# Two-layer graph attention on one core: the constant offset of layer 0's scores, written by ScalarE instead of by a product of ones

## What is computed

```
h = max(layernorm(x), 0)
x = x + L0(h, adj);  h = max(layernorm(x), 0);  x = x + L1(h, adj)

L0: e = (h Ws) (h Wt)^T ; z = where(adj > 0, e, -9e15) ; h' = softmax(z) (h Wc)
L1: Wh = h W ; e = leaky_relu(s1[:, None] + s2[None, :]) ; masked softmax ; elu(softmax @ Wh)
```

## Time and profile before

| | |
|---|---|
| median of 3 runs | 1403.41 us (1398.08 to 1406.76) |
| span of the profiled execution | 1402.6 us |
| busy: TensorE matmul, VectorE, ScalarE | 1276.6, 1250.6, 1024.8 us (91%, 89%, 73%) |
| DMA engines | 363.10 MB moved |

### The profile page before, as it was taken

How to read it: one execution, slowest core, us unless ns; L and a number is a source line. 1 busy time by engine, 2 the same in 40 slices (tenths; PEclk the granted TensorE clock), 3 DMA queues, 4 the chain that set the end, 5 groups by cost and what they waited for, 6 DMA issues and landing times.

```text
span 1402.6 us, 76097 instructions
## 1 busy us (share of the span) xinstructions
PE 1276.6 (91%) x31819; PEld 1131.9 (81%) x31947; DVE 1250.6 (89%) x2323; ACT 1024.8 (73%) x2036; POOL 32.3 (2%) x75
## 2 busy tenths in 40 slices
PE   5867899999999999999999999989899999999996
PEld 3656788888888888878878888877799999999995
DVE  8877799999999999989999999847899999999996
ACT  5755576767667677667676666748789999999994
POOL 2200000000000000000000000013000000000000
PEclk9979899999999999999999999999899999999998
DMA  6678899999999999999999999531134244334322
GB/s 249 248 266 287 280 345 369 370 381 368 368 391 357 377 378 366 383 380 341 382 378 361 376 374 374 223 114 55 56 108 121 81 124 123 108 94 123 117 85 72
DMA packets 104081, 363.10 MB, mean 259 GB/s; under 512 B 11520, under 2 KB 36352, under 8 KB 70144
## 3 DMA queue, kind: packets, MB, share of 16 engines
q1 hardware_dynamic: 103936, 361.02, 71.2%
HBM read 319.03 MB, written 41.94 MB: 257 GB/s over the span
## 4 chain that ended last, share of the span: by engine, by line
PE 46%; DMA 18%; DVE 16%; issue 12%; ACT 5%; SPq 1%; DVEq 1%; ACTq 0%; POOL 0%; POOLq 0%
DMA arena<-in_adjB 18%; PE ps L883 16%; PE ps L857 9%; DVE arena L1490 5%; PE ps L769 4%; DVE arena L1465 4%; PE ps L764 3%; PE ps L737 3%; DVE mx L1499 2%; ACT arena L1132 2%; PE ps L790 2%; PE ps L725 2%; PE ps L763 1%; PE ps L664 1%; SPq L434 1%
## 5 line engine op out<-in xcount | busy, mean ns | idle before, releaser
L790 PE MATMUL ps<-arena 128*128 128x129 f32 x2048 | 249.0, 280 | 0.4 <-issue 0.4
L1118 ACT ACTIVATE arena<-ps 128x512 f32<-128x512 f32 x256 | 153.2, 598 | 129.8 <-PE ps L737 129.8
L883 PE MATMUL ps<-arena 128*128 128x129 f32 x2048 | 245.1, 278 | 0.4 <-issue 0.4
L790 PEld LDWEIGHTS ps<-arena 128*128 128x128 f32 x2048 | 240.6, 196 | 0.6 <-issue 0.6
L1465 DVE TENSOR_SCALAR arena<-arena 128x2048 fp8e4<-128x2048 int32 x192 | 234.9, 1224 | 3.5 <-PE ps L752 1.5
L883 PEld LDWEIGHTS ps<-arena 128*128 128x128 f32 x2048 | 236.8, 194 | 0.5 <-issue 0.5
L1708 DVE TENSOR_SCALAR arena<-arena 128x128 f32<-128x128 f32 x768 | 202.4, 339 | 19.5 <-issue 14.3
L1112 ACT ACTIVATE arena<-ps 128x512 f16<-128x512 f32 x256 | 153.9, 601 | 52.5 <-PE ps L725 52.3
L769 PEld LDWEIGHTS ps<-arena 128*128 128x128 f16 x2048 | 137.5, 99 | 62.0 <-issue 2.2
L1499 DVE TENSOR_REDUCE mx<-ps 128x1 f32<-128x1024 f32 x128 | 155.7, 1216 | 29.9 <-PE ps L769 29.3
L737 PE MATMUL ps<-arena 128*32 128x128 f16 x8192 | 165.3, 223 | 16.5 <-issue 10.7
(11 more groups left out here) (165 smaller groups left out, 1400.4 us busy)
## 6 DMA issues: line engine op xcount, KB each, us to landing
arena<-in_adjB SPq DMA_DIRECT2D x256, 1024.0 KB, 7.3
sel_pick<-arena SPq DMA_DIRECT2D x64, 256.0 KB, 9.6
sel<-arena SPq DMA_DIRECT2D x64, 256.0 KB, 9.5
arena<-sel_pick SPq DMA_DIRECT2D x64, 256.0 KB, 3.8
arena<-sel SPq DMA_DIRECT2D x64, 256.0 KB, 2.8
arena<-in_xB SPq DMA_DIRECT2D x4, 1024.0 KB, 6.1
x_t<-in_x SPq DMA_DIRECT2D x64, 64.0 KB, 8.0
x_mid<-y_t SPq DMA_DIRECT2D x64, 64.0 KB, 8.3
```

Of the source, the lines that this page charges most:

```text
L790: last = nc.tensor.matmul(pv_ps, p_T[:, s * P:(s + 1) * P], v_sel[:, b, s, :], start=False, stop=(s == SB - 1), skip_group_check=True)
L883: last = nc.tensor.matmul(xv_ps[b], w_msk[:, b, s, :], x1_sel[:, b, s, 0:VW], start=False, stop=(s == SB - 1), skip_group_check=True)
```

## The change

From the second tile on, the product of ones is gone. ScalarE writes -2 OFF over the two banks it has just read, with a Copy of scale 0 and a constant bias, in place (`seed`), straight after each `exps`. TensorE's scores wait for `seeded` where they waited for `p_done`, and the mask product adds to what ScalarE wrote (`start=False`). The first tile keeps the product of ones. A semaphore `seeded` is added.

```diff
-                wait(pe, p_done, t * 2 + (q // 2 - 1))
                 dst = s_ps[q]
-                nc.tensor.matmul(dst, ones_b[:, :], negc, start=True, stop=False, skip_group_check=True)
+                if isinstance(t, int) and t == 0:
+                    nc.tensor.matmul(dst, ones_b[:, :], negc, start=True, stop=False, skip_group_check=True)
+                else:
+                    pe.wait_ge(seeded, t * 2 + (q // 2 - 1))
+                    settle()
                 nc.tensor.matmul(dst, off_i[q // 3], m_sel8[:, b, 4 * q:4 * q + 4, :].rearrange("p s n -> p (s n)"),
                                  start=False, stop=False, skip_group_check=True)
...
+            def seed(t, h):
+
+                act.wait_ge(p_done, t * 2 + (h + 1))
+                dst = ps[:, 2 * h:2 * h + 2, :].rearrange("p b n -> p (b n)")
+                nc.scalar.activation(dst, dst, ACT.Copy, bias=-2.0 * OFF, scale=0.0).then_inc(seeded, 1)
...
                 if there(i, 3):
                     exps(c, 0)
+                    seed(c, 0)
                 if there(i, 2):
                     take_values(a, b, 0)
                     take_keys(a, 3)
                 if there(i, 3):
                     exps(c, 1)
+                    seed(c, 1)
```

More of the change, by code:

```diff
@@ L283, in gnn_kernel @@
         p_done = sem("p_done")
+        seeded = sem("seeded")
         pv_done = sem("pv_done")
```

## The result

The changed kernel takes 1440.3 us (median of 4, 1439.2 to 1442.7) against 1404.0 us (median of 4): a ratio of 1.025, 95% interval 1.022 to 1.029. It is slower by 36 us; 1405 was forecast.

What follows compares the result with a forecast made beforehand. The prediction took memory traffic at 372 GB/s to fill the 13.01 us tile. Its sum was 1402.6 + 0 + 1 + 1 = 1404.6 us on the profiled span, 1405 on the median, own range 1400 to 1411, chance 0.60.

Steps and rivals of the forecast that it cites:

- What bounds the kernel: Steady tile of layer 0: memory traffic alone, 4.85 MB at 372 GB/s, was said to fill the 13.01 us.
- The second cover: Queue of DMA transfers: 4.1 us queued at the next tile's first issue, 3.3 after the change, so the tile stays 13.01.
- The first cover: ScalarE's wait for chunk 3's landing, 1.38 us a tile, was to absorb the 0.87 us longer lap, leaving 0.51.
- The walk of the path: One tile followed through ScalarE, TensorE and VectorE: two seeds of 1.03 us make the lap 0.87 us longer.
- the signs: What the new profile would show, such as seeds of 1.03 us, tiles of 13.0 us and DMA share 0.99.
- Removal of the product of ones: On TensorE: 252 products gone, 55 us of work or 0.88 us a tile, worth nothing by itself.
- The small terms: Steady tiles with short landing waits +1 us, laps behind the last landing +1, early tiles 0.
- Rival 1: Lap of ScalarE and TensorE: seed of 1.29 us or more outlasts the landing wait; nearly all near 1431 us; chance 0.10.
- Rival 2: Irregular landings and a thin DMA queue cost 0.1 to 0.3 us a tile, 1410 to 1422 us; chance 0.19.
- Rival 3: Less TensorE work shortens VectorE's wait for scores: faster, 1385 to 1399 us; chance 0.08.
- Rival 4: Mask product overwrites ScalarE's constant in PSUM: wrong rows at 1405 us, or many times longer in dense form; chance 0.03.

Runs made afterwards that it cites:

- dbl_b: The kernel before the change, with a second buffer for chunk 3 and its transfer issued right behind chunk 0: 1379.3 us, ratio 0.982.
- dbl_mid: The changed kernel with two buffers for chunk 3, which is issued behind chunk 1 and ahead of chunk 2: 1380.9 us, ratio 0.987.
- h1: The changed kernel with seeds for banks 2 and 3 only; banks 0 and 1 keep the product of ones: 1403.0 us, ratio 0.999.
- work2: The kernel before the change, plus two seed-sized copies a tile on ScalarE into SBUF that no other engine waits for: 1427.1 us, ratio 1.020.
- h0: The changed kernel with seeds for banks 0 and 1 only; banks 2 and 3 keep the product of ones: 1445.0 us, ratio 1.027.

## Why the prediction was wrong

**What bounds the kernel** was the step that failed first: "the memory traffic alone fills the tile". The prediction multiplied the tile by 372 GB/s and found the bytes that a tile moves. But 372 was measured in this tile: bytes over a rate taken from the same stretch give the stretch back, whatever binds. dbl_b moves the same bytes at 383 GB/s and dbl_mid at 386. The loop of 25.9 us in two tiles had been read off the chain and was the answer: 25.9 / 2 = 12.95.

What the runs showed in its place is a loop of waits without slack: 1 us of mean lap cost 0.64 us of tile in the changed kernel, and opening the loop gave 1379.3 us without the seeds and 1385.6 with them.

**The second cover** failed with it. "That queue is the cushion into which a longer compute chain can eat": the leg of 9.39 us did not shrink to pay for the seeds (9.54 and 10.02; in the mean 9.57 after 9.52). The likely reason, argued from the order of the issues and not measured: all four chunks of a tile are issued after the same row of conversions, so a delay moves them together, and what stands ahead of chunk 3 is mostly its own tile's chunks. The 4.1 us of queued work at the first issue were read off one tile; in others the queue ran dry (133 GB/s at 528 us).

**The first cover** failed in the same way. The walk of the path was near: seed 1.008 us (1.03 forecast), median lap longer by 1.02 us (0.87 forecast; the shortest laps went from 11.41 to 12.36). ScalarE's wait for the landing was to fall from 1.38 to 0.51 us. It fell to 1.04: the landing moved away as the lap grew, since it hangs on the lap of the tile before. A wait inside a loop is not slack. Of the signs, TensorE's wait for the seed came out at 61.7 us where more than 100 were forecast, and VectorE's wait for scores grew by 21 us, inside the 0.87 us a tile allowed for it.

**Removal of the product of ones**: no run takes it away alone. TensorE's busy time in the steady stretch fell, from 656.8 us of 702.6 to 622.8 of 709, and h1, with half of the products gone, gained nothing, as forecast.

**The small terms.** The early tiles came out 1.9 us shorter where 0 was forecast, and what follows the last landing 3.0 longer where +1 was.

**The rivals.** Rival 1 named the right lap, and put the point of decision at a cover that wasn't there. Rival 2 had the thin queue, and as forecast a tile over 13.2 us with ScalarE still waiting and the DMA rate down; but it stopped at 0.3 us a tile, and 0.64 were measured. Rival 3 didn't come: no rate of 384 GB/s without another order of issues. Rival 4 didn't come either: with seeds in all four banks the output is still the reference's, so the mask product added to ScalarE's constant, and layer 1 ran in its sparse form.

What stays open: why the transfer leg keeps its 9.5 us when the engines have gaps, and grows when less is moved; why a microsecond of mean lap costs 0.6 to 0.7 us of tile and not 0.5; and what limits once the loop is open. The 25 us of work2, forecast as 15, are nearly accounted for: the mean lap grew by 0.71 us and not by 0.55, and the tile by 0.42 us, which is 23 us in 54 tiles.

## What to carry to other kernels

When DMA engines look full, look for the loop: follow the chain that ended last from one issue to the same issue a round later, divide by the rounds it spans, and if that is the time of the round, expect to pay for what is put into it (here 0.6 to 0.7 us a tile for a microsecond in a loop of two tiles), whatever waits and queues lie in it. Never take the rate of a stretch as the ceiling of that same stretch. And a second buffer pays through the time of the issue it allows: here one buffer of 8 KB a partition and another order of four issues was worth 1.8%, and with it the same two seeds, which had cost 36 us, lie 6 us apart from the kernel without them, less than the measurement can tell for sure.

## What the hardware showed that was not expected

A Copy of 128 x 1024 numbers on ScalarE from PSUM to PSUM took 1008 ns, 102 less than the exps of the same shape into SBUF (1110 ns), in every one of 128. TensorE's granted clock fell to 0.50 after it had done nothing for 2.25 us (changed kernel, 518 to 520 us) and after 1.96 us of doing nothing and one bank of scores (h0), and was back at 1.00 after some 3 us in which it worked. The laps with a fall were longer than the others by some 1.2 us in h0 and by 0.5 to 0.7 in the changed kernel. And a load of half the bytes, in rows of half the length, ahead of a load of the full size, made that one land later, not earlier (10.36 us against 9.52 on the chain).
